# Attention products in fp32, one head per strip of 32 partitions, and feed-forward rows in pairs, in a one-core transformer layer

## The reference

```python
x = x + attn(layernorm(x)); x = x + ffn(layernorm(x))
# attention, 16 heads of 16 features
q, k, v = split(x @ W_qkv + b_qkv);  q = q / 4
score = einsum('bhqd,bhkd->bhqk', q, k) + einsum('bhqd,qkd->bhqk', q, pe_k)
attn  = softmax(score, axis=-1)
ctx   = einsum('bhqk,bhkd->bhqd', attn, v) + einsum('bhqk,qkd->bhqd', attn, pe_v)
return ctx @ W_out + b_out
# pe_k and pe_v are rows of tables of 129 relative distances, clipped at 64 both ways
# feed-forward: every operand goes through blockwise fp4 (blocks of 16) and back
return fp4_linear(silu(fp4_linear(x, w_gate)) * fp4_linear(x, w_up), w_down)   # 704 hidden
```

## Time and profile before

| | |
|---|---|
| median of 3 runs | 2285.17 us |
| the profiled execution | 2287.79 us, its span 2286.1 us |
| PE busy | 2187.2 us (96%) |
| DVE busy | 1897.4 us (83%) |
| ACT busy | 1394.6 us (61%) |
| POOL busy | 675.3 us (30%) |
| M products (L845) | 2048, mean 390 ns |
| far S products (L943) | 2176, mean 342 ns |
| mean granted TensorE clock | 0.978 of full speed |

### The profile page before, as it was taken

How to read it: one execution, slowest core, us unless ns; L and a number is a source line. 1 busy time by engine, 2 the same in 40 slices (tenths; PEclk the granted TensorE clock), 3 DMA queues, 4 the chain that set the end, 5 groups by cost and what they waited for, 6 DMA issues and landing times. The chain is left out here.

```text
span 2286.1 us, 51430 instructions
## 1 busy us (share of the span) xinstructions
PE 2187.2 (96%) x20396; PEld 1133.6 (50%) x20396; DVE 1897.4 (83%) x3615; ACT 1394.6 (61%) x2624; POOL 675.3 (30%) x483
## 2 busy tenths in 40 slices
PE   7989999999999999999999999999999987999997
PEld 4514445544444444444545444444444445666665
DVE  6687888888888888888888888888888716999997
ACT  3406767767777667776666677767677663444442
POOL 5503333333333333333333333333333320111111
PEclk9958999999999999999999999999999999999999
DMA  5743433433333344433333332334333201111110
GB/s 162 192 108 92 134 96 97 102 96 92 96 96 96 111 108 108 117 91 96 101 98 96 101 96 87 96 107 121 91 111 97 81 15 44 46 46 46 46 46 21
DMA packets 275676, 210.55 MB, mean 92 GB/s; under 512 B 17154, under 2 KB 266628, under 8 KB 275332
## 3 DMA queue, kind: packets, MB, share of 16 engines
q1 hardware_dynamic: 274308, 203.34, 32.5%
q0 software_dynamic: 1152, 4.19, 0.7%
HBM read 113.35 MB, written 93.34 MB: 90 GB/s over the span
## 5 line engine op out<-in xcount | busy, mean ns | idle before, releaser
L1139 DVE TENSOR_REDUCE amax<-psA 128x1 f32<-128x512 f32 x2048 | 1297.4, 684 | 203.6 <-PE psA L845 190.5
L1089 ACT ACTIVATE probs<-psS 128x512 f32<-128x512 f32 x1792 | 943.1, 610 | 337.2 <-PE psS L943 332.8
L845 PE MATMUL psA<-keys,queries 96*128 96x512 bf16 x2048 | 737.9, 390 | 2.0 <-DVE amax L1139 2.0
L943 PE MATMUL psS<-queries,keys 102*128 102x512 bf16 (+7 forms) x2176 | 586.1, 342 | 1.0 <-issue 0.3
L863 PE MATMUL psC<-probs,vals 128*32 128x512 f32 (+7 forms) x4352 | 476.5, 525 | 3.6 <-ACT probs L1089 2.2
L798 POOL TENSOR_TENSOR band_probs<-band_probs,side 128x2048 f32<-128x2048 f32 x64 | 288.8, 4533 | 494.7 <-PE psC L955 494.7
L845 PEld LDWEIGHTS psA<-keys,queries 96*128 96x128 bf16 x2048 | 190.8, 98 | 336.8 <-DVE amax L1139 224.4
L943 PEld LDWEIGHTS psS<-queries,keys 102*128 102x128 bf16 (+1 forms) x2176 | 203.2, 98 | 213.7 <-ACT probs L1089 47.1
L1084 ACT ACTIVATE band_probs<-psS 128x512 f32<-128x512 f32 x256 | 153.4, 600 | 132.8 <-PE psS L932 132.5
L863 PEld LDWEIGHTS psC<-probs,vals 128*32 128x32 f32 (+1 forms) x4352 | 89.2, 102 | 196.7 <-ACT probs L1089 111.7
L1460 PE MATMUL psG<-w_gate_up_T,f_xqT 128*128 128x352 f32 x512 | 159.8, 466 | 0.9 <-ACT f_xqT L1514 0.9
(11 more groups left out here) (161 smaller groups left out, 2057.0 us busy)
## 6 DMA issues: line engine op xcount, KB each, us to landing
rel_skew<-rel_scores SPq DMA_DIRECT2D x32, 2048.0 KB, 9.1
rel_near<-rel_skew SPq DMA_DIRECT2D x64, 1024.0 KB, 7.9
keys<-k_ring SPq DMA_DIRECT2D x48, 256.0 KB, 5.8
queries<-q_parts SPq DMA_DIRECT2D x192, 64.0 KB, 2.4
ctx_d<-rden SPq DMA_DIRECT2D x32, 256.0 KB, 2.3
ctx_in<-ctx_d SPq DMA_DIRECT2D x32, 256.0 KB, 2.7
q_parts<-parts SPq DMA_DIRECT2D x16, 384.0 KB, 3.0
k_ring<-parts SPq DMA_DIRECT2D x12, 384.0 KB, 3.3
```

Of the source, the lines that this page charges most:

```text
L845: t.matmul(small("M", m, n), qs[0:NR, qb, h, u * P:(u + 1) * P], keys[0:NR, par, h, c0:c0 + NQ], start=True, stop=True).then_inc(small_rea ...
L943: ins = t.matmul(bank[:, o:o + k], keys[0:nr, par, h, c0:c0 + P], qs[0:nr, qb, h, q0:q0 + k], start=True, stop=True, skip_group_check=True)
L1089: ins = a.activation(probs[:, n % 4, half], src, ACT.Exp)
L1139: v.reduce_max(amax[:, pair, k:k + 1], small("M", m, n), AX.X).then_inc(small_taken, 1)
```

## The change

Queries and keys stay fp32. A head's 16 rows stand at partitions 0, 32, 64 or 96 by its number in the group (`strip`), with two more rows for the shift; a score is an fp32 product of 17 or 18 rows, a maximum one of 16. The cuts into bf16 parts and their transfers are gone. The M products go by head in turn (`max_item`) and no longer through one head first. In the feed-forward stage, the first strand works on two tiles at once (512 features), and the weights of the last 64 hidden rows are padded with zeros to 128.

```diff
+STRIP = P // HG
+NRL, NRH = HD + 1, HD + 2
+def strip(h, rows):
+    return slice(STRIP * h, STRIP * h + rows)
...
-            def rest(n, bank):
...
-            def second(n, bank):
-                act.wait_ge(res_ready, n * BANKS + bank + 1)
-                a.copy(parts[:, bank, 1, :], res[:, bank, :]).then_inc(p2_ready, 1)
...
+                a.activation(qk[:, n % 2, bank, :], psP[:, bank, :], ACT.Identity, bias=bias[:, bank:bank + 1]).then_inc(qk_ready, 1)
...
-        self.rel_rows = sb("rel_rows", [NR, P], BF16)
+        self.rel_rows = sb("rel_rows", [P, P])
...
+def max_item(n):
+    return (n + 2) % HG, n // (HG * APER), n // HG % APER
...
-                for r, (cut, count) in enumerate(((m_pool, 3 * m + 1), (m_pool, 3 * m + 3), (shift_ready, m + 1))):
-                    wait_alone(sp, passed, cut, count)
-                    sp.dma_start(qs[NR + r:NRH:3, qb], shift[:, r, :]).then_inc(shift_in[qb], 16)
+                wait_alone(sp, passed, unit_done, emptied("T", m))
+                for r in range(2):
+                    sp.dma_start(qs[strips(HD + r), qb], shift[r * APAIRS:(r + 1) * APAIRS, :]).then_inc(shift_in[qb], 16)
...
-                t.matmul(small("M", m, n), qs[0:NR, qb, h, u * P:(u + 1) * P], keys[0:NR, par, h, c0:c0 + NQ],
+                t.matmul(small("M", m, n), qs[strip(h, HD), qb, u * P:(u + 1) * P], keys[strip(h, HD), par, c0:c0 + NQ],
...
-                        ins = t.matmul(bank[:, o:o + k], keys[0:nr, par, h, c0:c0 + P],
-                                       qs[0:nr, qb, h, q0:q0 + k], start=True, stop=True, skip_group_check=True)
+                        ins = t.matmul(bank[:, o:o + k], keys[strip(h, nr), par, c0:c0 + P],
+                                       qs[strip(h, nr), qb, q0:q0 + k], start=True, stop=True, skip_group_check=True)
...
-        self.keys = ctx.enter_context(nc.sbuf_tensor("keys", [NRH, 2, HG, S], BF16))
-        self.qs = ctx.enter_context(nc.sbuf_tensor("queries", [NRH, QB, HG, NQ], BF16))
+        self.keys = ctx.enter_context(nc.sbuf_tensor("keys", [P, 2, S], F32))
+        self.qs = ctx.enter_context(nc.sbuf_tensor("queries", [P, QB, NQ], F32))
...
-        DVE_ORDER = "HXHXHXHXHHHXXHXXHXXXXXXXXHY"
+        FIRST_X, LAST_X = 13, 6
+        ODD, EVEN = "HYXHXXHXXHXHHHHXXHXXHXXX", "HYXHXHXHXHXHXHHHH"
...
-                v.tensor_add(x1[:, r], psO[:, 0:D], xr[:, k]).then_inc(x1_ready, 1)
+                v.tensor_add(x1[:, p % 4], psO[:], xr[:, k]).then_inc(x1_ready, 1)
```

More of the change, by code:

```diff
@@ L44, with strips @@
 EPS = 1e-5
[L47 to L52, removed]
+STRIP = P // HG
+NRL, NRH = HD + 1, HD + 2
+def strip(h, rows):
+    return slice(STRIP * h, STRIP * h + rows)
+def strips(row):
+    return slice(row, P, STRIP)
 VC = HD + 2
@@ L125, in projections, with stores_of @@
     last = 2 * R
-    def stores_of(bank, n):
-        return 16 * (n + (n // NBLK if bank >= 2 else 0))
+    def stores_of(bank, q, n):
+        return 16 * sum(2 if bank >= 2 and m % NBLK == NBLK - 1 else 1 for m in range(q, n, 2))
     with ExitStack() as ctx:
@@ L319, in _ @@
                 more = n + 1 < N
-                first(n, 0)
-                first(n, 1)
+                rows(n, 0)
+                rows(n, 1)
                 if more:
                     deviation(n + 1)
-                second(n, 0)
-                first(n, 2)
-                second(n, 1)
-                first(n, 3)
-                second(n, 2)
+                rows(n, 2)
                 if more:
                     turned(n + 1)
-                second(n, 3)
+                rows(n, 3)
         @block.vector
@@ L417, in _ @@
                     moments(n + 1)
-                rest(n, 0)
-                if more:
                     normalise(n + 1)
-                for bank in range(1, BANKS):
-                    rest(n, bank)
                 values(n)
@@ L732, in iteration @@
                     load_queries(g2, qb2)
-                if qb < 3 and not last:
+                if qb < 2 and not last:
                     wait_alone(sp, passed, keys_in, (g * KDMAS + KDMAS + 2 * qb) * 16)
@@ L1137, in take @@
                 ready("M", m, n)
-                pair, k = divmod(n, APER)
+                h, u, k = max_item(n)
+                pair = h * CH + u
                 v.reduce_max(amax[:, pair, k:k + 1], small("M", m, n), AX.X).then_inc(small_taken, 1)
@@ L1430, in _, with store @@
+            def store(m):
+                wait_alone(sp, passed, y_ready, m + 1)
+                sp.dma_start(of[m * P:(m + 1) * P, :], yo[:, m % 2]).then_inc(y_out[m % 2], 16)
+            for p in range(4):
+                load(p)
+            for n in range(NT):
+                if n % 2 and (n + 7) // 2 < NP:
+                    load((n + 7) // 2)
+                if n >= 2:
+                    store(n - 2)
+            for m in range(NT - 2, NT):
+                store(m)
             for k in range(2):
-                sp.wait_ge(y_out[k], 16 * (NT // 2 + 1))
+                sp.wait_ge(y_out[k], 16 * (NT // 2))
@@ L1504, in _ @@
+            project(4)
+            for n in range(NT):
+                if n + 1 < NT:
+                    gate_up(n + 1)
+                if n:
+                    down(n - 1)
+                if n + 5 < NT:
+                    project(n + 5)
+                if n + 2 < NT:
+                    turn_x(n + 2)
+                turn_h(n)
+            down(NT - 1)
         @block.scalar
@@ L1544, in _ @@
+            turned_x(1)
+            for n in range(NT):
+                if n % 2 and (n + 3) // 2 < NP:
+                    deviation((n + 3) // 2)
+                if n + 1 < NT:
+                    gated(n + 1)
+                if n + 2 < NT:
+                    turned_x(n + 2)
+                turned_h(n)
         @block.vector
```

450 lines of the change are left out of this document (196 added, 254 removed).

## The result

The changed kernel takes **4764.74 us**, the median of 4 runs (4716.64 to 4777.94), the kernel before 2284.18 in the runs beside it: ratio **2.0814**, 95% interval 2.0666 to 2.0963 (ratios here and below are taken over all runs; the two medians alone give 2.086). 3100 us was forecast, 3600 was the end of the range. The profiled execution took 4763.33 us, its span is 4761.6.

The account below looks back on a forecast made before the run. PE was taken to bound attention: an iteration goes from 53.0 to 79.8 us, +831 over 31; with first maxima +10, shift -2, projections -9, feed-forward -17 that is +813 on 2287.8, said as 3100 us, range 2700 to 3600.

Parts of the forecast that it names:

- The clock falls: Rival for attention: 16-row products may keep PE's granted clock at the lower level, 155 us an iteration, 5450 us; chance 0.04.
- here it has always something queued: Argument against a falling clock in attention: PE always has work queued, unlike in the first maxima where DVE held it back.
- Strips run beside each other: Attention: up to four fp32 products in different row strips cost as much as one, 0.88 us.
- round: Attention's pricing unit: up to four products, one per strip, at 0.88 us; 52 an iteration, 45.8 us in place of 28.6.
- The work of an iteration: Attention: 45.8 + 24.4 + 2.2 + 3.9 + 3.5 = 79.8 us, 26.8 more than 53.0; +831 us over 31 iterations.
- Banks: Attention: in seven blocks the fourth maximum waits for DVE to read the first, 0.5 us each, 3.5 us an iteration.
- Whole-array work that overlaps the strips: Rival for attention: full-array pieces start strip by strip, 53.4 us an iteration, about 2260 us, faster; chance 0.08.
- two changes and the loads: Attention: 22 changes between strips and whole array at 0.1 us, 2.2; strip weight loads 0.15 in 26 blocks, 3.9.
- First maxima: Maxima ahead of the iterations: longer at a clock of 0.50, 0 to +20 us for 75 maxima, +10 taken.
- Projections: Projections stage: without the bf16 cuts PE holds 11.7 us a block, about 1.2 us x 7; -9 us, 0 to -12.
- Feed-forward: Feed-forward stage: fewer DVE instructions, step 11.38 to 10.7 us, -21, +4 for the first pair; net -17, -28 to 0.
- The last iteration: End of attention: no maxima there and four scores fill a round, so the sum covers only 31 iterations.

Follow-up runs that it names:

- Experiment 2: Changed kernel with every maximum and score product reading all 32 rows of its strip, rows 18 to 31 zeros; 3359.91 us, 1.4701 of before.
- experiment 5: Pieces of an iteration run as products alone, behind full products or products that leave the clock low; four strips of 16 rows behind the latter: 69 us for 40 rounds.
- experiment 1: Products alone, one kind per stretch behind 20 full products, output a copy of the input; 40 rounds of four 16-row strips took 34.62 us.
- experiment 4: Changed kernel with the earlier order of maxima, through one head first, 77 rounds by count for 52; 6280.45 us.
- experiment 6: Changed kernel with another step table and order of maxima, 35 rounds by count for 52, products still of 16 to 18 rows; 3977.99 and 4135.75 us.
- experiment 7: Changed kernel with the step table and order of maxima of experiment 6 and the 32-row reads of Experiment 2; 3033.92 us, 1.3257 of before.
- Experiment 9: The 32-row kernel of Experiment 2 with four banks for maxima and three for scores, instead of three and four; 3538.97 us.

## Why the prediction was wrong

- **The step that failed** is the silent one: 79.8 us an iteration were priced at a granted clock of 1.00. "The clock falls" stood among the rivals at 0.04 and 5450 us, and was set aside with "here it has always something queued". PE did have something queued, busy 3943 of 3970 us, and was at 0.58 all the same. Experiment 2 gives back 1405 us with the products in the same order, and experiment 5 shows near blocks at the lower level with no wait at all. The 0.50 of the first maxima in the earlier trace rows was no evidence either way: a stream of 96-row products without waits keeps the upper level (160 in 34.70 us, experiment 1), so the reason given for it may be right there, but it says nothing of streams of 16 rows.
- **The rival's mechanism was right, its size half right.** It had the lower level throughout, 155 us; the kernel spends part of each iteration at the upper one, 132.3 us at a mean of 0.58.
- **Strips run beside each other**, at 0.865 us a round: right, and shown alone. The Trainium skill ("TensorE: Matmul & The Clock Gate", Part 3, Packing small matmuls) has 3.07x for four such products; here 40 rounds of four cost 34.62 us where 40 full products cost 34.50, so 4x.
- **The work of an iteration**, 79.8 predicted: 76.7 by the changed kernel's clock, 81.6 with 32 rows. The sum was right within 4%, and adding 25 rounds cost 20 us (experiment 4). Taking 17 away did not save 15: the same prices give 60.4 us for 35 rounds, and the two kernels with them need 71 and 77.4 (experiments 6 and 7). So the formula is not sound in general, and part of the agreement at 52 rounds may be luck.
- **Banks**, 3.5 us: right in kind, its size not measured. In experiment 7 the weight loads of M wait 169.3 us for DVE in some 28 iterations, 6 us in each, and those of S as long for ACT. Experiment 9 can't size the term for the changed order, since the scores' waits took its place.
- **Whole-array work that overlaps the strips**: no. Transposes and four strips take 1.65 us in experiment 5. Four transposes (0.11 each) and a round would be 1.30 apart, and the other 0.35 is what the prediction had for two changes and the loads. (That rival's 2260 takes the most that the other terms give back, 40 us; with the 18 of the forecast it is 2282.)
- **First maxima**, 0 to +20 us, +10 taken: +26.3, at the lower level (0.97 for an M; 0.87 was the end of the range). The prediction had 1.76 us for a product at that level; one that runs alone takes 2.07 (at 2094.20), and 2.07 + 0.16 + 0.69 over three banks is 0.97, an estimate that fits. **Projections** -9: a block of 11.55 us where 11.7 was forecast, and the first M starts 9.8 us earlier. Together +16.5 to the first T, for -1 forecast.
- **Feed-forward** -17, 0 to -28: -36 in the kernel after, -34 alone. The term was too small: a step is 10.17 us, not 10.7, with PE's groups end to end. PE's own work fell below the 10.5 read from the earlier trace rows. The six products down (twelve records), the last of 64 rows before and padded to 128 now, took 2.88 us (2056.98 to 2059.86) and take 2.59 (4528.74 to 4531.33), and the projection behind them 1.73 for 1.83. The prediction had nothing for the padding; that it is the padding was not tested alone.
- **The last iteration** was left out of the sum (nothing for M, "four S fill a round"); it took 43 us more, at 0.68 of the clock.

With the measured clock the prediction's own sum is 79.8 / 0.58 = 137.6 us an iteration and about 4890 us in all (2288 + 31 x 84.6 - 18), 3% over the 4765 measured: the clock is by far the largest thing that it had wrong.

## What to carry to other kernels

Price PE's work twice, at both levels of its clock, as soon as a change makes products read fewer rows of the array; a busy PE is no evidence that the clock stays. Where rows can be filled with zeros at no price, read the whole strip. Before packing four heads beside each other, count the rounds between whole-array work, and then how long each product holds its PSUM bank: four in parallel at a quarter of the pace keep the throughput, and their banks stay taken longer.

## What was not expected of the hardware

- Four strips of 16 rows keep a clock of 1.00 (34.62 us for 40 rounds) and can't raise one of 0.50 (69 us); four strips of 32 rows raise it (37 us), and so do products of 17 columns over all rows (37 us). Two strips of 32 rows keep it too (34.60) and don't raise it (69).
- Rows that hold only zeros count for the clock: 0.93 when rows 18 to 31 are read, 0.58 when they are not.
- Two runs of the same program, experiment 6, differ by 158 us with their mean clocks, 0.704 and 0.671, on a kernel that sits between the levels.
- Four fp32 products in strips cost what one full product costs, 0.865 against 0.863 us.
